# Two LayerNorms of a software-pipelined decoder layer: from VectorE at the end of a body to ScalarE at the start of the next

## The reference

```python
x = layernorm(x + attn(x))          # 3 heads, softmax over the *queries*, mean of the heads, fc
x = layernorm(x + xattn(x, ctx))    # 16 heads of 32, causal, keys and values from a 128-wide context
x = layernorm(x + ffn(x))           # top 6 of 64 experts (capacity 128) and a shared expert

def layernorm(x, eps=1e-5):
    return (x - mean(x)) / sqrt(var(x) + eps)
```

## Time and profile before

| | |
|---|---|
| median of 3 runs | 2461.53 us (2461.4 to 2464.21) |
| span of the profiled execution | 2453.7 us (its own time is this and what lies around it) |
| PE busy | 2105.3 us, 86% |
| VectorE busy | 1763.2 us, 72% |
| ScalarE busy | 979.3 us, 40% |
| GpSimd busy | 800.1 us, 33% |
| mean granted TensorE clock | 0.925 of full speed |

### The profile page before, as it was taken

The page is one execution under the profiler, slowest core; times in us unless marked ns, Lnnn a source line. Parts: engine busy times, 40 slices in busy tenths (PEclk is TensorE's granted clock), DMA queues, the critical chain, the costliest instruction groups (busy, mean ns, idle before and its releaser), DMA issues. The chain is left out here.

```text
span 2453.7 us, 50213 instructions
## 1 busy us (share of the span) xinstructions
PE 2105.3 (86%) x17648; PEld 1323.7 (54%) x17648; DVE 1763.2 (72%) x3784; ACT 979.3 (40%) x1515; POOL 800.1 (33%) x637
## 2 busy tenths in 40 slices
PE   7988899889889989988988963499999999999940
PEld 3555565555556556556555642266666666666620
DVE  5457877787777778778777776567777777777758
ACT  4323333342343333334244332355555554545423
POOL 1012313322421331332242122434454444444443
PEclk9999999899999989989999985599999999999975
DMA  6801011011001101101100012387878787878753
GB/s 214 179 31 37 2 36 37 0 36 36 9 28 36 36 0 36 36 0 36 36 9 28 19 70 70 92 245 232 252 230 255 236 248 232 253 232 253 232 179 148
DMA packets 132885, 268.71 MB, mean 110 GB/s; under 512 B 32304, under 2 KB 42544, under 8 KB 132848
## 3 DMA queue, kind: packets, MB, share of 16 engines
q1 hardware_dynamic: 108176, 226.13, 28.3%
q0 software_dynamic: 20480, 33.71, 6.8%
q10 hardware_dynamic: 4192, 8.39, 0.9%
HBM read 217.12 MB, written 51.12 MB: 109 GB/s over the span
## 5 line engine op out<-in xcount | busy, mean ns | idle before, releaser
L830 ACT ACTIVATE x_plus_shared<-ring 128x512 f16<-128x512 f32 x224 | 131.3, 593 | 420.6 <-PE ring L659 405.4
L633 POOL TENSOR_SCALAR_AFFINE_SELECT x_plus_shared<-x_plus_shared 128x1024 f32<-128x1024 f32 x64 | 71.3, 1115 | 678.6 <-ACT x_plus_shared L846 678.4
L659 PE MATMUL ring<-tion_then_expert_weights,xT_split 128*128 128x512 f16 x1152 | 291.9, 410 | 0.8 <-DVE cross_out L963 0.3
L659 PE MATMUL ring<-xT_split,tion_then_expert_weights 128*128 128x256 f16 x2304 | 266.4, 274 | 3.7 <-PEq L240 3.7
L107 POOL DMA_INDIRECT slot_table<-table_records,slot_of_choice x192 | 220.8, 1150 | 144.2 <-DVE slot_of_choice L1031 59.5
L659 PEld LDWEIGHTS ring<-xT_split,tion_then_expert_weights 128*128 128x128 f16 x2304 | 222.5, 98 | 41.2 <-issue 12.1
L910 DVE SCALAR_TENSOR_TENSOR x_plus_shared<-ring,x_plus_shared 128x512 f16<-128x512 f32 x192 | 129.5, 686 | 126.7 <-ACT x_plus_shared L830 117.5
L659 PEld LDWEIGHTS ring<-tion_then_expert_weights,xT_split 128*128 128x128 f16 x1152 | 116.3, 104 | 150.9 <-issue 43.2
L1187 POOL DMA_INDIRECT expert_sums<-tion_then_expert_weights,scatter_index x64 | 149.0, 2328 | 59.0 <-POOL scatter_index L1184 55.7
L948 DVE CUSTOM_DVE_ANT_0 quad<-quad,causal_penalty 128x128 f32<-128x128 f32 (+1 forms) x512 | 164.4, 394 | 4.6 <-PE quad L729 2.3
L659 PE MATMUL ring<-x_plus_shared,weights_split 128*128 128x512 f16 x576 | 134.8, 390 | 28.4 <-DVE weights_split L924 28.4
(11 more groups left out here) (198 smaller groups left out, 4219.1 us busy)
## 6 DMA issues: line engine op xcount, KB each, us to landing
tion_then_expert_weights<-in_w_gate SPq DMA_DIRECT2D x64, 704.0 KB
tion_then_expert_weights<-in_w_up SPq DMA_DIRECT2D x64, 704.0 KB
tion_then_expert_weights<-in_w_down SPq DMA_DIRECT2D x64, 512.0 KB, 4.0
tion_then_expert_weights<-in_w_down SPq DMA_DIRECT2D x64, 192.0 KB, 4.3
xT_in<-in_xT SPq DMA_DIRECT2D x16, 512.0 KB, 4.5
x_in<-in_x SPq DMA_DIRECT2D x16, 512.0 KB, 5.0
expert_sums<-zero_rows SPq DMA_DIRECT2D x16, 512.0 KB, 10.6
x_rows<-x_plus_shared SPq DMA_DIRECT2D x16, 512.0 KB, 2.8
```

The lines of the kernel that those rows point to most:

```text
L633: pool.affine_select(out=p32[:, g % 2, :, 0:2 * P], in_=p32[:, g % 2, :, 0:2 * P], compare_op=ALU.is_ge, fill=0.0, base=0, pattern=[[0, 4] ...
L659: last = pe.matmul(out_, left(a, c), right(b, c), start=(n == 0), stop=(n == 3 * chunks - 1))
L830: act.activation(half(0), src, ACT.Copy, scale=scale).then_inc(high, 1)
```

## The change

The one list `BODY` becomes four, `PE_BODY`, `ACT_BODY`, `DVE_BODY` and `POOL_BODY`. With one exception the order of the steps of each engine is as it was. Where a wait counted banks filled or freed by a place in the common list, it now counts by the place in PE's list (`job`) or VectorE's list (`freed`); the numbers stand for the same steps. The exception is the norm:

- LN on VectorE ends after the scales: four `tensor_scalar` go, one small `scalar_tensor_tensor` comes, which writes the shift, -mean x scale, for all rows.
- NX1 on ScalarE, after Y1's split of the next body, writes x1 with two `Identity`. NX2, after T1's split and ahead of K0's, writes x2 with two more.
- VectorE no longer waits for the store of x2 before LN, ScalarE does before NX2. O0 waits for NX1 and OUT0 for NX2 before `pre` and `pre2` are written again. POOL's x + bias waits for O1's evacuation in the last body instead of `ln1`. AV waits for VectorE's own last AV.

```diff
+ACT_BODY = [
+    ("Y", 0, 0), ("Y", 0, 1), ("NX1", 0, 0), ("V", 0, 0), ("V", 0, 1), ("T", 0, 0), ("T", 1, 0),
+    ("NX2", 0, 0), ("K", 0, 0), ("K", 1, 0), ("TX", 0, 0), ("TX", 1, 0), ("Q", 0, 0), ("Q", 1, 0),
...
         @block.scalar
         def _(act):
             def emit(b):
-                for s in b.steps:
+                for s in b.act:
                     name, g, h = s
-                    if s in b.split:
+                    if name == "NX1":
+                        act.wait_ge(scaled, b.i)
+                        for t in range(NB):
+                            last = act.activation(x1[:, t, :], pre[:, t, :], ACT.Identity,
+                                                  scale=rstd[:, t:t + 1], bias=shift[:, t:t + 1])
+                        last.then_inc(ln1, 1)
+                    elif name == "NX2":
+                        act.wait_ge(scaled, b.i)
+                        act.wait_ge(x2_stored, b.n(0, 0, 16, 1))
+                        for t in range(NB):
+                            last = act.activation(x2[:, t, :], pre2[:, t, :], ACT.Identity,
+                                                  scale=rstd[:, NB + t:NB + t + 1], bias=shift[:, NB + t:NB + t + 1])
+                        last.then_inc(ln2, 1)
+                    elif s in b.split:
...
-                    for n, src, dst in rows:
-                        last = dve.tensor_scalar(dst, src, mv[:, n, 0:1], rstd[:, n:n + 1], ALU.subtract, ALU.mult)
-                        if n % NB == NB - 1:
-                            last.then_inc(parts[(n - n0) // NB][3], 1)
+                    dve.scalar_tensor_tensor(shift[:, n0:n1], mv[:, n0:n1, 0], -1.0, rstd[:, n0:n1],
+                                             ALU.mult, ALU.mult).then_inc(scaled, 1)
...
                         if g == 0:
                             dve.wait_ge(xb_ready, b.n(1, 0, 0, 1))
+                            if b.b:
+                                dve.wait_ge(ln1, b.n(0, 1, 0, 1))
...
                         if b.b:
-                            dve.wait_ge(free, b.job("OUT", 1, 0))
-                            dve.wait_ge(x2_stored, b.n(0, 0, 16, 17 if b.c else 1))
-                            parts.append((NB, pre2, x2, ln2))
-                        norm(parts)
+                            dve.wait_ge(free, b.freed("OUT", 1, 0))
+                            rows += [(NB + t, pre2[:, t, :]) for t in range(NB)]
+                        row_scales(rows)
...
                     elif name == "AV":
                         dve.wait_ge(full, b.job(*s))
+                        if g > 0:
+                            dve.wait_ge(free, b.freed("AV", g - 1, 0))
...
                     elif name == "OUT":
                         dve.wait_ge(full, b.job(*s))
+                        if b.c and g == 0:
+                            dve.wait_ge(ln2, b.n(0, 0, 1, 1))
...
-                    if not b.is_(0):
-                        pool.wait_ge(ln1, b.n(1, 0, 0, 0))
+                        if not b.is_(0):
+                            pool.wait_ge(free, b.last_freed("O", 1, 0))
```

More of the change, by code:

```diff
@@ L494, in __init__ @@
             self.c = not (isinstance(i, int) and i < 2)
[L495 to L498, removed]
+            self.pe, self.act, self.dve, self.pool = (
+                self.own(order) for order in (PE_BODY, ACT_BODY, DVE_BODY, POOL_BODY))
+            self.ring = [s for s in self.pe if s[0] in RING_STEPS]
@@ new lines, in __init__, with own @@
+            self.split = [s for s in self.act if s[0] in SPLIT_STEPS]
+            self.freed_order = [f for s in self.dve
+                                for f in ([("S", s[1], 0), ("S", s[1], 1)] if s[0] == "S1" else
+                                          [s] if s[0] in RING_STEPS and s[0] != "S" else [])]
+            assert sorted(self.freed_order) == sorted(self.ring)
+        def own(self, order):
+            return [s for s in order if
+                    (self.a if s[0] in A_STEPS else self.c if s[0] in C_STEPS else
+                     self.a or self.b if s[0] == "LN" else self.b)]
@@ L500, in is_, with before, base, freed @@
         def is_(self, i):
             return isinstance(self.i, int) and self.i == i
+        def before(self):
+            return [Body(self.i - 1)] if isinstance(self.i, int) else [Body(1), Body(2)]
+        def base(self):
+            return done_before(self.i, RING_A, RING_B, RING_C)
         def job(self, *step):
-            return done_before(self.i, RING_A, RING_B, RING_C) + (self.ring[step] + 1)
+            return self.base() + (self.ring.index(step) + 1)
+        def freed(self, *step):
+            return self.base() + (self.freed_order.index(step) + 1)
@@ L507, in last_job, with last_freed @@
         def last_job(self, *step):
-            steps = [s for s in BODY if s in FULL(BODY) and (s[0] in A_STEPS or not self.is_(1))]
-            after = len(steps) - 1 - steps.index(step)
-            return done_before(self.i, RING_A, RING_B, RING_C) - after
+            return self.base() - min(len(p.ring) - 1 - p.ring.index(step) for p in self.before())
+        def last_freed(self, *step):
+            return self.base() - min(len(p.freed_order) - 1 - p.freed_order.index(step) for p in self.before())
@@ L513, in high @@
         def high(self, *step):
-            return done_before(self.i, 12, 8, 2) + (self.split[step] + 1)
+            return done_before(self.i, 12, 8, 2) + (self.split.index(step) + 1)
         def n(self, per_a, per_b, per_c, extra):
@@ L519, in bank @@
         def bank(self, *step):
-            return bank[self.ring[step] % RING]
+            return bank[self.ring.index(step) % RING]
         def reuse(self, eng, *step):
-            j = self.ring[step]
-            if not (self.is_(0) and j < RING):
-                eng.wait_ge(free, done_before(self.i, RING_A, RING_B, RING_C) + (j - RING + 1))
+            j = self.ring.index(step)
+            if j >= RING:
+                eng.wait_ge(free, self.freed(*self.ring[j - RING]))
+            elif not self.is_(0):
+                eng.wait_ge(free, self.base() - min(len(p.ring) - 1 - p.freed_order.index(p.ring[j - RING])
+                                                    for p in self.before()))
     def bodies(eng, emit):
@@ L664, in emit @@
             def emit(b):
-                for s in b.steps:
+                for s in b.pe:
                     name, g, h = s
@@ L879, in link, with row_scales @@
                     dve.wait_ge(dve_step, done_before(b.i, LINKS_A, LINKS_B, LINKS_C) + b.i * LINKS_LN + (1 + links[0]))
-                def norm(parts):
-                    rows = [(at + t, pre[:, t, :], dst[:, t, :]) for at, pre, dst, _ in parts for t in range(NB)]
-                    for n, src, _ in rows:
+                def row_scales(rows):
+                    for n, src in rows:
                         last = dve.bn_stats(stats[:, n, :], src)
@@ L887, in norm @@
                     own_wait(dve, taken)
-                    for n, _, _ in rows:
+                    for n, _ in rows:
                         last = dve.bn_aggr(mv[:, n, :], stats[:, n, :])
```

120 lines of the change are left out of this document (64 added, 56 removed), and 26 rows, old and new, of tables (ACT_BODY, BODY, DVE_BODY, PE_BODY).

## The result

The changed kernel takes 2493.8 us (median of 4 runs, 2491.2 to 2494.9) against 2461.5 (4 runs, 2461.4 to 2464.2): a ratio of 1.0125, 95% interval 1.0111 to 1.0139. It is slower, as forecast, but by 32 us and not by 17, and lies just outside the range. The profiled executions stand 35.8 us apart (the page's first line of the changed kernel, against the earlier trace rows); in later runs the time is 1.7 us above the span, so the profiled execution of the kernel before was some 6 us shorter than its median, and that of the changed kernel 2.6.

What follows compares the result with a forecast made beforehand. The prediction took the seam between bodies to be bound by PE, with a tie at Q0; 15.4 + 1.1 + 0.7 = 17.2 us lengthen the span from 2453.7 to 2470.9, plus 7.8 around it: 2479, range 2467 to 2492.

Steps and rivals of the forecast that it cites:

- The seam: Where one body meets the next: NX2 ahead of K0's split makes Q0 1.1 us late, 15.4 us over 14 bodies.
- VectorE's saving: VectorE's norm gets 2.8 us shorter per body, but this only turns into idle time: 0 us gained.
- NX1 hidden: In the seam, x1 on ScalarE is ready at 753.8, T0 wants it at 755.96: 2.1 us of cover, no cost.
- POOL's earlier start: POOL's x + bias starts about 12 us earlier, while VectorE waits for OUT; worth nothing either way.
- Both sides move together and nothing gives the 1.1 us back.: Behind Q0, PE's waits for VectorE's maxima (2.27 us a body) shift along, so none of Q0's delay is recovered.
- The clock's term: Head 1's S at the lower clock: six of 14 bodies kept, 1.67 us each; three to ten possible, -5 to +7 us.
- Rival 1: The new pause ahead of TX0 also drops the clock at TX and Q: 12 to 23 us more, 2491; chance 0.14.
- Bodies 16 and 17: Behind the 14 full bodies: Q0 of body 16 1.1 us later, TX of body 17 0.7 us later.
- The 7.8 us around the span: Median of the runs over the profiled span, 2461.53 against 2453.7, added again to the forecast span of 2470.9.

Runs made afterwards that it cites:

- e2: The kernel before with two dummy Identity of 128x512 on ScalarE behind T1's split, TX0 not waiting for them; ratio 1.0060 to the kernel before.
- e1: The changed kernel with NX2 moved between the splits of V0 and V1 on ScalarE; ratio 1.0019 to the kernel before.
- e4: The changed kernel with only x1 written by ScalarE, x2 by VectorE as before; ratio 1.0018 to the kernel before.
- e18: The changed kernel with four added matmuls of 128x64 ahead of TX0's wait; ratio 1.0065 to the kernel before.
- e7: The kernel before with two dummy Identity of 128x512 behind T1's split on ScalarE and TX0 waiting for them; ratio 1.0102 to the kernel before.
- e17: The changed kernel with six added matmuls of 128x64 ahead of M3's wait; ratio 1.0009 to the kernel before.

## Why the prediction was wrong in size

- *The seam, 15.4 us.* Right: 1.07 a body, 15.0 us. NX2's 1.52 us between T1's and K0's splits, PE's pause ahead of TX0 (0.82, released by ScalarE), Q0 right behind K0's second half, VectorE still idle for 1.93 us before Q1: all as said, and e2 priced it by itself.
- *VectorE's saving, 0 us; NX1 hidden; POOL's earlier start, nothing.* Right (e1, e4).
- *"Both sides move together and nothing gives the 1.1 us back."* Right up to AV1. What failed is what it took for granted, that behind Q0 a body is the old one, merely later. It is not: OUT is slow in 12 of the 14 bodies, 20.0 us. With 0.15 a body more in the chain of P, 2.1 us, that makes 15.0 + 20.0 + 2.1 = 37.1 against 38.3 measured. Of the 1.2 left, 1.0 lies in body 2, which differs from the usual body in both kernels.
- *The clock's term, "I leave it at six", -5 to +7 us.* This is the step that failed, and the term that was mis-sized: it came to +20. It looked at head 1's S alone, and for that it was right, six before and six after. The 20 us are OUT's, at the lower clock behind a pause that had grown from 1.33 to 2.3 us and more. The trace of the kernel before had a warning in it: in every body 7 to 10 us at a granted clock of 0.50 behind AV1 (in the one shown 717.3 to 727.3), which I did not price because it was hidden.
- *Rival 1* had the right size (12 to 23 us) and the wrong place. I looked for the lower clock at TX and Q, which run at the full rate, and argued it away with OUT's full rate ahead of the seam. That OUT ran at full rate behind 1.33 us of pause said nothing about a longer pause there, and the change made it longer. The range reached 2492 for this rival's sake, so that the miss by 2 us is small by luck: the forecast's own mechanism gave 2479.
- *The Trainium skill*, "TensorE: Matmul & The Clock Gate", section "HAM oscillation — how this bites in real kernels", says that pauses bring the half clock and are each paid for again. The trace agrees that it is paid again in each body, and at OUT it is paid right behind a pause, one that has grown from 1.33 to 2.30 us. It does not agree for the new pause of 0.82 us ahead of TX0: behind it PE is at full rate, and e18 keeps 0.70 us of it without the price.
- *Bodies 16 and 17, 1.1 + 0.7.* From norm to T0 0.71 more in body 16, the wait of TX 0.70 longer in body 17: right. Q0 of body 16 is 1.66 late in place of 1.1, and not as worked out: K and TX there take 2.77 and 1.71 us (2.44 and 1.04 before), at a granted clock of 0.51 (1487 to 1493.8 us). In e4, which has no NX2, Q0 is nearly as far behind T0 (5.79 us against 5.84). The tail is 2.6 us longer in place of 1.8.
- *The 7.8 us around the span* were no such thing. In the runs since, time and span lie 1.7 us apart; the profiled execution was shorter than the median one.

## What to carry to other kernels

A step moved to another engine goes where that engine has a gap *and nobody behind it is on the path*: three places earlier in the list NX2 is free (e1), between T1 and K0 it costs 1% and more. When a moved step puts a pause on the matrix engine, price the delay by the seam, and then look up where the kernel now runs at the lower clock without paying for it, and which of its pauses would grow; the lower clock on an exposed stage was the larger half of the bill here. A few cheap matmuls into a free bank inside a wait are worth one run in such a kernel: six of them gave 0.7% here.

## What the runs showed of the hardware

- Two `Identity` of 128x512 from SBUF with scale and bias per row take 1.52 us in a pair on ScalarE, in the seam as in the earlier trace rows.
- PE can stall in front of small row-tiled matmuls for 0.2 to 0.5 us at a time with nothing to wait for that the profile shows, 15 to 25 us over 14 bodies, in the last of four like groups of a body; and a program may lose or regain this by an edit 49 us away (e2 and e7).
- OUT's 24 matmuls of 128x512 took 5.34 us behind every pause of less than 1.9 us (194 bodies), and 6.8 to 7.04 in 65 of the 86 bodies with a longer one.
- Six matmuls of 64 columns (0.34 us) ahead of a wait of 1.47 us kept the next product at the upper clock level, 2.4 GHz (S 2.79 us in 14 of 14 bodies), where without them it fell to 1.2 GHz in six of 14 (e17 and the changed kernel).
- The time of one body changed with the clock mostly in steps of 1.67 us (S at 4.46 in place of 2.79) and 1.69 us (OUT at 7.03 in place of 5.34), so a few us of difference between two programs need a count of such steps beside the ratio.
